# Statistics of all sixteen normalisations counted in the stages that make the rows

## The chip, the cores and the metric

The kernel runs on one core of a Trainium2 chip, as one program in fp32. The metric is the device time of one execution in microseconds (us); the median of three runs is shown.

## What is computed

A network of four layers on `x` of 128 sequences by 32 positions by 128 channels (4096 tokens of 128 values), with a second input `ctx_2048` of 128 by 257 by 256. Each layer has three blocks (cross attention, attention, feed-forward), and each of the twelve adds to `x` what it computes from the normalised `x`:

```python
def _layernorm(x, axis=-1, eps=1e-05):
    m = jnp.mean(x, axis=axis, keepdims=True)
    v = jnp.var(x, axis=axis, keepdims=True)
    return (x - m) / jnp.sqrt(v + eps)
...
    x = x + _L0_xattn_ref(_layernorm(x, axis=-1), ctx_2048, ...)
    x = x + _L0_attn_ref(_layernorm(x, axis=-1), ...)
    ...
    x = x + _L3_ffn_ref(_layernorm(x, axis=-1), L3_ffn_W1, L3_ffn_b1, L3_ffn_W2, L3_ffn_b2)
```

Some blocks normalise once more inside: the output of layer 0's cross attention, the row before layer 2's channel mixing (`x` after its RWKV recurrence), and twice in layer 2's feed-forward. That makes sixteen normalisations, each over the 128 channels of every token.

## The kernel before

The rows lie in SBUF for the whole program: `X` is 128 partitions by 32 tiles of 128 channels, a chunk is four tiles (512 columns), so there are eight chunks. `XT` holds the normalised rows turned over, channel by token, as the matmuls need them. Each block of a layer is one or more stages; a stage ends with a barrier of all engines, and buffers of a stage are its own.

`normalise` (L113 to L407) is a stage of its own, called sixteen times under the names n0x, n0y, n0a, n0f (layer 0), d1n, n1a, n1f, n2x, n2a, n2b, n2f, n2g, n2h, d3n, n3a, n3f. VectorE (DVE) runs `bn_stats` (L198) on each of the 32 tiles, which leaves six numbers per row; `variances` (L204 to L216) makes mean and variance of them in seven small instructions; ScalarE (ACT) takes the root (L334, with a warming activation at L365 and a table load ahead of it); `invert` (L227 to L240) makes the scale and one Newton step in six small instructions of DVE; then the rows are written as (x + nmean) * scale, on DVE (L250) or ACT (L346), turned over by TensorE (PE, L403) and stored to `XT` by DVE (L283, L285) or ACT (L361). This is done in two parts, tiles 0 to 15 and 16 to 31 (`PARTS`), so that the first part is written while the second is counted. The order on DVE is written out by hand:

```python
                take(*PARTS[0])
                variances(0)
                lo, hi = PARTS[1]
                take(lo, lo + 4)
                invert(0)
                take(lo + 4, hi)
                variances(1)
```

Kinds of `normalise`: with gain and bias as columns (`by_cols`, applied at the store); with gain and bias as rows (`by_rows`), where `affine` multiplies and adds them on DVE (L267, L272); with `add_to` (n0y, n2h), where POOL adds the bias rows to `X` (L315) and DVE adds the product; `whole` (n2g), which keeps the normalised rows in `H` and turns them over too; and with `keep` or `residual` and `twice` (n2a, n1f), where each tile is written a second time.

The rows that a normalisation counts were made by the stage ahead of it, always with a last addition on DVE: `mixture` (f0, f2: four `scalar_tensor_tensor` per expert at L654, f2 into `H`), `depooled` (d1, d3: L756), `layer1_attn` (m: L1007), `network` (f2a: L1191), `layer2_attn` (r: ACT stores `H` of a chunk at L1405 after `mix` of DVE, L1492 to L1508), `layer3_attn` (a: L1768), `project` (bp: L1845, into `H`), `layer2_xattn` (x), `landmark_read` (y: L3430), `gated_mixture` (g: L4400), `context_attention` (c: ACT writes `att`, L3978) and, for the first, the DMA that loads `X`, beside which `context_weights` runs. In f0, f2, d1, d3, f2a, bp, and in most of c and x, the chunks are passes of a loop, whose addresses are computed at run time. In the first normalisation SyncE (SP) issues 16 small DMAs (L3471, `store_rows`) for the next stage.

Of the kernel before, what the change touches and what calls it, by code (L numbers as in the profile page):

```python
# [20 lines left out]
ds = bass.ds  # L21

B, S, D = 128, 32, 128
TOK = B * S
P = 128
# [86 lines left out]

def normalise(k, name, src, gain=None, bias=None, twice=False, keep=None,  # L113
              add_to=None, residual=False, whole=False, eps=EPS, fetch=None):
# [6 lines left out]
    PARTS = ((0, 16), (16, TILES))  # L121
    BANKS = 4
    with ctx:
        sb, ps = buffers(nc, ctx)
        stats = sb(f"{name}_stats", [P, TILES, 6])
# [54 lines left out]

        with nc.Block() as block:
# [13 lines left out]
            def _(v):  # L195
# [46 lines left out]
                def apply(c):  # L242
# [3 lines left out]
                    if turning and c >= BANKS:  # L246
                        v.wait_ge(turned, c - BANKS + 1)
                    for t in range(TC):
                        n = c * TC + t
                        v.tensor_scalar(out[:, t], tile_of(src, n), nmean[:, n:n + 1], scale[:, n:n + 1],  # L250
                                        ALU.add, ALU.mult).then_inc(applied[c], 1)
                    if residual:
                        v.wait_ge(extra, part_of(c))
                    for t in range(TC):
# [4 lines left out]
                        elif keep is not None and twice:  # L259
# [3 lines left out]
                def affine(c):  # L263
# [22 lines left out]

                take(*PARTS[0])
                variances(0)
                lo, hi = PARTS[1]
                take(lo, lo + 4)  # L290
                invert(0)
                take(lo + 4, hi)
                variances(1)
                if by_rows or by_cols:
                    v.wait_ge(loaded, 32 if by_rows or bias else 16)
                if by_rows:
                    affine(0)
                    invert(1)
                    for c in range(1, CHUNKS):
                        affine(c)  # L300
                else:
                    apply(3)
                    invert(1)
                    apply(4)
                    store(3)
                    apply(6)
                    apply(7)
                    store(7)
# [21 lines left out]
            def _(act):  # L330
# [5 lines left out]
                def apply(c):  # L336
# [7 lines left out]
                    for t in range(TC):  # L344
                        n = c * TC + t
                        act.activation(out[:, t], tile_of(src, n), ACT.Identity, scale=scale[:, n:n + 1],  # L346
                                       bias=shift[:, 0, n:n + 1]).then_inc(applied[c], 1)
                    if both:
                        act.wait_ge(extra, part_of(c))
# [4194 lines left out]
```

## Time and profile before

| | us |
|---|---|
| median of 3 runs | 4563.62 (4560.72 to 4564.95) |
| profiled execution, whole | 4552.12 |
| its span, first to last instruction | 4550.3 |
| PE busy in the span | 3768.0 (83%) |
| DVE busy | 2792.0 (61%) |
| ACT busy | 2084.2 (46%) |
| POOL busy | 864.0 (19%) |
| mean granted clock of PE | 0.910 |

The profiled execution took 1.8 us more than its span, and 11.5 us less than the median of the runs. Busy shares are means over stages of very different kinds; PE's clock is given as a share of 2.4 GHz.

### The profile page before, as it was taken

What the parts mean: (1) busy time and instruction counts of PE and PEld (TensorE: products, weight loads), DVE (VectorE), ACT (ScalarE), POOL (GpSimd) and SP (SyncE); (2) the same over time, 40 slices, a digit from 0 to 9 for tenths busy, and PEclk for the clock granted to TensorE, in tenths of its full rate; (3) what the DMA queues carried; (4) which work ended last, traced back from release to release, by engine and by line L of the source; (5) the groups of instructions that cost most, each with busy time, mean ns of one, the idle gap of its engine ahead of it and who ended that gap; (6) DMA issues with size and microseconds to landing.
All of it is one profiled execution on the core that took longest, in us unless ns stands there. A gap on an engine that the chain in (4) does not pass through costs nothing. (4 is left out here: it accounts for less than half of the span.)

```text
span 4550.3 us, 86911 instructions
## 1 busy us (share of the span) xinstructions
PE 3768.0 (83%) x31478; PEld 2724.4 (60%) x31478; DVE 2792.0 (61%) x5475; ACT 2084.2 (46%) x4489; POOL 864.0 (19%) x832
## 2 busy tenths in 40 slices
PE   7999999999999471499996689799996777868376
PEld 6777777777777241366665356566663355646254
DVE  4666656565665686522224866477777927867783
ACT  2333333333333455444433444488887646654323
POOL 0000000000000231200001046455561022200360
PEclk8999999999999785699997889899997898989668
DMA  3111111111111145400000023122220000000000
GB/s 108 48 47 47 47 47 48 49 54 47 47 47 43 31 142 161 172 2 0 0 0 25 20 113 149 64 68 67 67 76 8 0 5 3 0 13 0 9 2 24
DMA packets 203051, 215.97 MB, mean 47 GB/s; under 512 B 37328, under 2 KB 190896, under 8 KB 195376
## 3 DMA queue, kind: packets, MB, share of 16 engines
q1 hardware_dynamic: 202800, 212.63, 14.8%
q8 instruction: 157, 2.57, 0.2%
q14 instruction: 94, 0.77, 0.1%
HBM read 185.26 MB, written 27.05 MB: 47 GB/s over the span
## 5 line engine op out<-in xcount | busy, mean ns | idle before, releaser
L3864 PE MATMUL c_psO<-c_pt,c_vc 128*128 128x512 f32 x1024 | 485.5, 596 | 2.5 <-ACT c_ot L3973 2.5
L3836 PE MATMUL c_psS<-c_kc,c_qt 128*128 128x257 f32 x2048 | 465.9, 380 | 1.1 <-DVE c_qt L4012 1.1
L3965 ACT ACTIVATE c_sc<-c_psS,c_mx 128x257 f32<-128x257 f32 x512 | 215.3, 473 | 486.6 <-DVE c_mx L4030 486.6
L3836 PEld LDWEIGHTS c_psS<-c_kc,c_qt 128*128 128x128 f32 x2048 | 381.2, 190 | 67.0 <-issue 17.5
L590 ACT ACTIVATE f_hT<-f_psH,f_b_up 128x512 f32<-128x512 f32 x320 | 214.1, 688 | 280.7 <-PE f_psH L537 275.7
L547 PEld LDWEIGHTS f_psY<-f_w_down,f_hT 128*128 128x128 f32 x2560 | 302.3, 192 | 63.9 <-issue 50.2
L537 PE MATMUL f_psH<-f_xs,f_w_up 128*128 128x512 f32 x640 | 301.5, 606 | 18.5 <-ACT f_hT L590 18.5
L3821 PEld LDWEIGHTS c_psQ<-XT,c_m 128*128 128x128 f32 x1984 | 259.8, 191 | 94.2 <-issue 90.7
L547 PE MATMUL f_psY<-f_w_down,f_hT 128*128 128x128 f32 x2560 | 305.4, 275 | 10.2 <-ACT f_hT L590 7.0
L2256 POOL TENSOR_TENSOR x_sc<-x_sc,x_rec 128x1156 f32<-128x1156 f32 x128 | 270.6, 2114 | 207.4 <-DVE x_rec L2522 207.4
L3973 ACT ACTIVATE c_ot<-c_psO 128x512 f32<-128x512 f32 x256 | 153.0, 598 | 342.3 <-PE c_psO L3864 342.3
L654 DVE SCALAR_TENSOR_TENSOR X<-f_psY,f_wt,X 128x128 f32 x256 | 72.1, 344 | 370.2 <-PE f_psY L547 370.2
L4012 DVE COPY c_qt<-c_psQ 128x512 f32<-128x512 f32 x248 | 169.4, 683 | 205.9 <-PE c_psQ L3821 205.9
L2450 ACT ACTIVATE x_sc<-x_psS,x_mx 128x289 f32<-128x289 f32 x512 | 250.0, 501 | 74.9 <-DVE x_mx L2499 74.9
L3780 POOL COPY c_z<-c_sc 128x8 f32<-128x8 f32 x128 | 24.6, 192 | 1348.3 <-DVE c_sc L4042 1348.3
L4026 DVE TENSOR_REDUCE c_nm<-c_psS 128x2 f32<-128x514 f32 x256 | 177.5, 693 | 142.9 <-PE c_psS L3836 138.3
L3821 PE MATMUL c_psQ<-XT,c_m 128*128 (+1 forms) x1984 | 261.6, 275 | 2.8 <-DVE c_qt L4012 2.8
L3864 PEld LDWEIGHTS c_psO<-c_pt,c_vc 128*128 128x128 f32 x1024 | 174.9, 190 | 133.6 <-issue 132.8
L2328 PE MATMUL x_psT<-ident,x_sc 128*128 128x128 f32 (+1 forms) x1536 | 216.4, 277 | 19.0 <-DVE x_pt L2506 12.5
L2499 DVE TENSOR_REDUCE x_mx<-x_psS 128x2 f32<-128x578 f32 x256 | 182.4, 753 | 76.6 <-PE x_psS L2313 76.4
L2328 PEld LDWEIGHTS x_psT<-ident,x_sc 128*128 128x128 f32 (+1 forms) x1536 | 159.0, 131 | 87.6 <-issue 87.4
L4255 POOL TENSOR_TENSOR g_hT<-g_gate,g_wide 128x512 f32<-128x512 f32 x128 | 173.2, 1365 | 111.7 <-ACT g_gate L4345 90.1
(816 smaller groups left out, 7683.9 us busy)
## 6 DMA issues: line engine op xcount, KB each, us to landing
c_kc<-in_ctxT SPq DMA_DIRECT2D x128, 257.0 KB
c_vc<-in_ctx SPq DMA_DIRECT2D x128, 256.0 KB
g_wide<-g_w_dram SPq DMA_DIRECT2D x32, 1024.0 KB, 8.5
x_kc<-in_ctxT SPq DMA_DIRECT2D x32, 512.0 KB
x_vc<-in_ctx SPq DMA_DIRECT2D x64, 256.0 KB
l_k_dram<-l_dist SPq DMA_DIRECT2D x32, 256.0 KB, 4.0
l_q_dram<-l_turn SPq DMA_DIRECT2D x8, 1024.0 KB, 9.8
y_pt<-l_q_dram SPq DMA_DIRECT2D x8, 1024.0 KB, 6.5
```

The source lines that it names most:

```text
L537: pe.matmul(psH[:, n % BANKS, :], w_up[:, n, :], xs[:, b, :], start=True, stop=True).then_inc(up_done, 1)
L547: mm = pe.matmul(psY[:, e % YB, t * P:(t + 1) * P], hT[:, n % SLOTS, t * P:(t + 1) * P], w_down[:, n, :], start=(u == 0), stop=(u == UT - 1))
L590: act.activation(hT[:, n % SLOTS, :], psH[:, n % BANKS, :], ACT.Gelu, bias=b_up[:, n:n + 1]).then_inc(act_done, 1)
L2256: g.tensor_tensor(sc[:, slot], sc[:, slot], bcast(rec[:, slot], 2, NK), ALU.mult).then_inc(scaled, 1)
L2328: mm = pe.transpose(psT[0:width, bank, r * P:(r + 1) * P], sc[:, c % SC, r, t * P:t * P + width], k.ident[:])
L2450: act.activation(sc[:, b % SC, r], psS[:, r, 0:NK], ACT.Exp, bias=mx[:, b % 2, r:r + 1], accum_out=sm[:, b % SC, r:r + 1]).then_inc(exp_do ...
L2499: v.tensor_reduce(two, psS[:, half * 2:half * 2 + 2, 0:NK], AX, ALU.max, negate=True)\
L3821: mm = pe.matmul(bank[:, q * P:(q + 1) * P], w["m"][:, four * 4 + q, half * P:(half + 1) * P], k.XT[:, ds(m * P, P)], start=True, stop=True)
L3836: mm = pe.matmul(psS[:, r, 0:KEYS], qt[:, b // BT, half, b % BT, r * G:(r + 1) * G].rearrange("p h i -> p (h i)"), kc[:, b // 2 % 2, b % 2 ...
L3864: mm = pe.matmul(psO[:], vc[:, slot, c % 2, t, half * P:(half + 1) * P], pt[:, c % 2, t], start=(t == 0), stop=(t == 1))
L3965: act.activation(sc[:, b % 2, r, 0:KEYS], psS[:, r, 0:KEYS], ACT.Exp, bias=mx[:, b % 2, r:r + 1]).then_inc(exp_done, 1)
L4026: v.tensor_reduce(nm[:, b % 2, two * 2:two * 2 + 2], psS[:, two * 2:two * 2 + 2, 0:KEYS], AX, ALU.max, negate=True).then_inc(reduced, 1)
```

## The change

`count_chunk` issues the four `bn_stats` of a chunk into one buffer `k.stats`, which lives as long as `X`. Every stage that makes rows calls it (or one `bn_stats` per tile, in x and c) on DVE behind its last addition to a chunk, after a wait for that addition. `normalise` is `counted=True` everywhere: it has no `bn_stats`, one part of 32 tiles, and so one `variances`, one root and one `invert`. `apply` is split into `write` (rows out) and `hold` (the second write). DVE writes chunks 0, 2, 3, 4, 6, 7 where it wrote 3, 4, 6, 7, ACT writes 1 and 5; in the `whole` kind DVE takes writes 0, 3 and 6 from ACT. The small DMAs in the first normalisation become 4 of equal total size. In layer 2's recurrence chunk j-2 is counted between `sums(j)` and `mix(j-1)`, behind a wait for ACT's store of it (`h_stored`); chunk 6 ahead of `mix(7)`, chunk 7 behind it. In `context_weights` each half of `X` is counted behind a wait for its load, ahead of the last copy of the weights (L3608 before) and of the copy of `nrow` (L3610 before). Of the thirteen places the diff below shows four; in the others the lines `v.wait_ge(added, ...)` and `count_chunk(v, k, k.X, c)` stand behind the addition named above. In `normalise` itself `affine` counts what it has added to `X` for the next one (n0a, d3n).

```diff
+def count_chunk(v, k, src, c):
+
+    for t in range(TC):
+        v.bn_stats(k.stats[:, ds(c * TC + t, 1), :], src[:, ds(c * CHUNK + t * P, P)])
...
+              add_to=None, residual=False, whole=False, eps=EPS, fetch=None, counted=True):
...
-    PARTS = ((0, 16), (16, TILES))
+    PARTS = ((0, TILES),) if counted else ((0, 16), (16, TILES))
...
-        stats = sb(f"{name}_stats", [P, TILES, 6])
+        stats = k.stats
...
+        holds = residual or (keep is not None and twice)
...
-                    v.wait_ge(stats_done, hi)
+                    if not counted:
+                        v.wait_ge(stats_done, hi)
...
+                        v.wait_ge(finished, c + 1)
+                        count_chunk(v, k, add_to, c)
...
+                    variances(0)
+                    invert(0)
+                    if by_rows:
+                        if whole:
+                            write(0)
+                        v.wait_ge(loaded, 32)
+                        for c in range(CHUNKS):
+                            affine(c)
+                            if whole and c in (0, 3):
+                                write(c + 3)
+                    else:
+                        write(0)
+                        write(2)
+                        write(3)
+                        write(4)
+                        if holds:
+                            hold(0)
+                        write(6)
+                        if by_cols:
+                            v.wait_ge(loaded, 32 if bias else 16)
+                        store(3)
+                        if holds:
+                            hold(2)
+                        write(7)
+                        if holds:
+                            hold(3)
+                            hold(6)
+                        store(7)
+                        if holds:
+                            hold(7)
...
+                elif whole:
+                    write(1)
+                    write(2)
+                    store(0)
+                    write(4)
+                    store(1)
+                    write(5)
+                    store(2)
+                    store(3)
+                    write(7)
+                    for c in range(4, CHUNKS):
+                        store(c)
+                elif by_rows:
+                    for c in range(CHUNKS):
+                        write(c)
+                else:
+                    write(1)
+                    store(0)
+                    store(1)
+                    write(5)
+                    store(2)
+                    if holds:
+                        hold(1)
+                    store(4)
+                    store(5)
+                    if holds:
+                        hold(5)
+                    store(6)
+                    if holds:
+                        hold(4)
...
+                        count_chunk(v, k, dest, c)
...
+                    if j >= 2:
+                        v.wait_ge(h_stored, j - 1)
+                        count_chunk(v, k, k.H, j - 2)
                     if j:
                         mix(j - 1)
+                v.wait_ge(h_stored, CHUNKS - 1)
+                count_chunk(v, k, k.H, CHUNKS - 2)
                 mix(CHUNKS - 1)
+                v.wait_ge(h_stored, CHUNKS)
+                count_chunk(v, k, k.H, CHUNKS - 1)
...
-                    for b in range(BT):
-                        for q in range(4):
-                            sp.dma_start(nv_dram[q, b].unsqueeze(0),
-                                         nrow[q % 2:q % 2 + 1].rearrange("o (r q d) -> o r q d", r=4, d=D)[:, :, q // 2])\
-                                .then_inc(weights_stored, 16)
-                    sp.wait_ge(weights_stored, (BT * 4 + 1) * 16)
+                    for q in range(4):
+                        row = nrow[q % 2:q % 2 + 1, q // 2 * 4 * D:(q // 2 + 1) * 4 * D]
+                        sp.dma_start(nv_dram[q].rearrange("b r d -> b (r d)").unsqueeze(0),
+                                     bcast(row, 1, BT)).then_inc(weights_stored, 16)
+                    sp.wait_ge(weights_stored, 5 * 16)
...
+                    if j == N_AT:
+                        v.wait_ge(k.x_in, 32)
+                        for c in range(CHUNKS // 2, CHUNKS):
+                            count_chunk(v, k, k.X, c)
...
+                def count_out(m):
+                    v.wait_ge(out_read, m + 1)
+                    v.bn_stats(k.stats[:, ds(m, 1), :], att[:, ds(m * D, D)])
...
+                        if b % BT == 1 and not first:
+                            count_out(m - 2)
```

**Order on DVE at the start of the first normalisation.** Before, the first ten rows of its stage; the second group of `bn_stats` lies between the two chains:

```order
L198 BN_STATS n0x_stats<-X 128x6 x16
L204 TENSOR_TENSOR n0x_diff<-n0x_stats 128x16
L205 TENSOR_TENSOR n0x_sums<-n0x_stats 128x16
L206 TENSOR_TENSOR n0x_nmean<-n0x_stats 128x16
L208 SCALAR_TENSOR_TENSOR n0x_diff<-n0x_diff 128x16
L211 SCALAR_TENSOR_TENSOR n0x_var<-n0x_sums,n0x_diff 128x16
L213 TENSOR_SCALAR n0x_nmean<-n0x_nmean 128x16
L216 TENSOR_SCALAR n0x_var<-n0x_var 128x16
L198 BN_STATS n0x_stats<-X 128x6 x4
L227 RECIPROCAL n0x_rs<-n0x_root 128x16
```

With the change, eight rows of the same stage; the chain now takes 32 columns at once:

```order
L213 TENSOR_TENSOR n0x_diff<-stats 128x32
L214 TENSOR_TENSOR n0x_sums<-stats 128x32
L215 TENSOR_TENSOR n0x_nmean<-stats 128x32
L217 SCALAR_TENSOR_TENSOR n0x_diff<-n0x_diff 128x32
L220 SCALAR_TENSOR_TENSOR n0x_var<-n0x_sums,n0x_diff 128x32
L222 TENSOR_SCALAR n0x_nmean<-n0x_nmean 128x32
L225 TENSOR_SCALAR n0x_var<-n0x_var 128x32
L236 RECIPROCAL n0x_rs<-n0x_root 128x32
```

The counting left this stage, and nothing stands between `variances` and the reciprocal.

**Order on DVE at the end of the recurrence of layer 2** (r; L1492 to L1508 are `mix`, whose lines are L1564 to L1580 with the change). Before, from the last row of `sums(7)` over `mix(6)` to the start of `mix(7)`:

```order
L1483 TENSOR_TENSOR r_past<-r_e,r_num 128x32x31
L1492 TENSOR_TENSOR r_cross<-r_lows 128x512
L1494 TENSOR_TENSOR r_ahead<-r_psU,r_lows 128x512
L1495 TENSOR_TENSOR r_back<-r_psU,r_lows 128x512
L1497 RECIPROCAL r_cross<-r_cross 128x512
L1499 TENSOR_TENSOR r_ahead<-r_ahead,r_back 128x512
L1502 SCALAR_TENSOR_TENSOR r_ahead<-r_ahead,r_sig 128x512
L1508 TENSOR_TENSOR r_mixed<-r_ahead,r_cross 128x512
L1492 TENSOR_TENSOR r_cross<-r_lows 128x512
```

With the change, the same stretch:

```order
L1555 TENSOR_TENSOR r_past<-r_e,r_num 128x32x31
L116 BN_STATS stats<-H 128x6 x4
L1564 TENSOR_TENSOR r_cross<-r_lows 128x512
L1566 TENSOR_TENSOR r_ahead<-r_psU,r_lows 128x512
L1567 TENSOR_TENSOR r_back<-r_psU,r_lows 128x512
L1569 RECIPROCAL r_cross<-r_cross 128x512
L1571 TENSOR_TENSOR r_ahead<-r_ahead,r_back 128x512
L1574 SCALAR_TENSOR_TENSOR r_ahead<-r_ahead,r_sig 128x512
L1580 TENSOR_TENSOR r_mixed<-r_ahead,r_cross 128x512
L116 BN_STATS stats<-H 128x6 x4
L1564 TENSOR_TENSOR r_cross<-r_lows 128x512
```

The count of chunk 5 came ahead of `mix(6)`, and that of chunk 6, which waits for ACT's store of it, ahead of `mix(7)`.

**Order on DVE between two chunks of f0** (ISA and REGISTER_ALU rows compute addresses of the loop; `f_lg` are the router's logits). Before:

```order
L654 SCALAR_TENSOR_TENSOR X<-f_psY,f_wt,X 128x128 x4
L603 REGISTER_ALU
L608 COPY f_lg<-f_psR 128x32
L53 ISA
L413 TENSOR_TENSOR f_gt<-f_lg 128x256
```

With the change:

```order
L719 SCALAR_TENSOR_TENSOR X<-f_psY,f_wt,X 128x128 x4
L116 ISA
L116 BN_STATS stats<-X 128x6
L116 ISA
L116 BN_STATS stats<-X 128x6
L116 ISA
L116 BN_STATS stats<-X 128x6
L116 ISA
L116 BN_STATS stats<-X 128x6
L668 REGISTER_ALU
L673 COPY f_lg<-f_psR 128x32
L53 ISA
```

The four `bn_stats` of the finished chunk, each behind a row for its address, stand ahead of the router's work for the next.

## Rows read from the trace of the kernel before

**Rows 1.** Page, busy time, share of span and instructions per engine

```profile
PE 3768.0 (83%) x31478; PEld 2724.4 (60%) x31478; DVE 2792.0 (61%) x5475; ACT 2084.2 (46%) x4489; POOL 864.0 (19%) x832
```

**Rows 2.** Line L198: idle us of DVE ahead of it, and times

```profile
  PEq L89: 24.8, 16
```

**Rows 3.** Windows: n0a, n0y, end of n0f's load, n1f, n2g, c, m, r

```profile
core 0: us, PE busy (x) PEld busy (x) DVE busy (x) ACT busy (x) POOL busy (x), PEclk, DMA share, GB/s
1529.60:1547.30 17.70, 6.80 (x32) 5.11 (x32) 15.57 (x76) 9.90 (x25) 0.00 (x0) 0.58 0.21 49
1500.00:1528.40 28.40, 0.00 (x0) 0.00 (x0) 27.58 (x74) 14.33 (x36) 9.87 (x8) 0.56 0.02 5
1932.60:1935.60 3.00, 2.48 (x12) 2.09 (x12) 2.13 (x8) 2.35 (x6) 0.00 (x0) 0.50 0.55 235
2599.20:2622.10 22.90, 7.87 (x32) 6.18 (x32) 20.32 (x94) 17.64 (x42) 0.94 (x4) 0.57 0.30 100
4029.70:4059.10 29.40, 8.92 (x32) 5.73 (x32) 20.91 (x74) 19.02 (x44) 0.00 (x0) 0.50 0.14 42
500.00:1000.00 500.00, 500.00 (x3077) 383.94 (x3076) 302.91 (x527) 164.65 (x374) 13.04 (x56) 1.00 0.16 48
2573.00:2599.00 26.00, 21.73 (x124) 16.08 (x123) 22.55 (x36) 0.16 (x1) 0.00 (x0) 0.93 0.00 0
3500.00:3650.00 150.00, 115.47 (x270) 51.64 (x270) 142.82 (x114) 99.21 (x118) 0.00 (x0) 0.89 0.00 0
```

**Rows 4.** Timeline of n0a: start, us, engine, line, operation, idle before

```profile
1529.63 3.19 DVE L198 BATCH_NORM_STATS2 n0a_stats<-X 128x6 f32<-128x128 f32 x16 [1.26 <-PEq L89]
...
1533.84 0.22 ACT L334 ACTIVATE n0a_root<-n0a_var 128x16 f32<-128x16 f32 x1 [4.02 <-DVE n0a_var L216]
...
1535.53 0.17 DVE L240 TENSOR_TENSOR n0a_shift<-n0a_nmean,n0a_rs 128x16 f32<-128x16 f32 x1
...
1535.62 2.41 DVE L198 BATCH_NORM_STATS2 n0a_stats<-X 128x6 f32<-128x128 f32 x12
1535.74 3.18 ACT L346 ACTIVATE n0a_xn<-X,n0a_shift,n0a_rs 128x128 f32<-128x128 f32 x8 [1.69 <-DVE n0a_shift L240]
...
1543.71 2.13 DVE L250 TENSOR_SCALAR n0a_xn<-X,n0a_nmean,n0a_rs 128x128 f32<-128x128 f32 x8
...
1546.60 0.69 DVE L285 COPY XT<-n0a_psT 128x512 f32<-128x512 f32 x1 [0.75 <-PE n0a_psT L403]
```

**Rows 5.** Timeline of n0x and of the end of context_weights

```profile
28.71 1.21 DVE L3610 COPY d_nrow<-d_psW 2x1024 f32<-2x1024 f32 x1 [2.79 <-PE d_psW L3571]
...
30.66 1.28 ACT L365 ACT_TABLE_LOAD   x1 [3.57 <-PEq L89]
...
31.43 11.51 SPq L3471 DMA_DIRECT2D c_nv_dram<-d_nrow  x16
31.95 0.20 ACT L365 ACTIVATE n0x_root<-ident 1x1 f32<-1x1 f32 x1
```

**Rows 6.** Timeline of n0y while POOL adds the bias rows

```profile
1503.39 3.77 POOL L315 TENSOR_TENSOR X<-X,n0y_rows 128x512 f32<-128x512 f32 x3 [19.63 <-DMA n0y_rows<-in_L_xattn_ln_bias]
...
1504.83 1.12 DVE L211 SCALAR_TENSOR_TENSOR n0y_var<-n0y_sums,n0y_diff 128x16 f32<-128x16 f32 x1
...
1507.11 0.86 DVE L198 BATCH_NORM_STATS2 n0y_stats<-c_att 128x6 f32<-128x128 f32 x4
```

**Rows 7.** Timeline of f0 between two chunks

```profile
2002.57 1.12 DVE L654 SCALAR_TENSOR_TENSOR X<-f_psY,f_wt,X 128x128 f32 x4 [2.45 <-PE f_psY L547]
...
2009.54 1.55 PE L537 MATMUL f_psH<-f_xs,f_w_up 128*128 128x512 f32 x3 [2.68 <-ACT f_hT L590]
```

**Rows 8.** Timeline of r around the start of `mix(7)`

```profile
3638.41 0.69 DVE L1492 TENSOR_TENSOR r_cross<-r_lows 128x512 f32<-128x512 f32 x1
...
3639.55 0.60 ACT L1405 ACTIVATE H<-r_psO 128x512 f32<-128x512 f32 x1 [4.59 <-PE r_psO L1343]
```

**Rows 9.** Timeline of y (behind an addition) and of bp

```profile
1897.05 0.23 DVE L3413 TENSOR_SCALAR y_rec<-y_psO 128x64 f32<-128x64 f32 x1 [1.21 <-PE y_psO L3386]
...
4018.63 0.69 DVE L1841 TENSOR_TENSOR bp_rows<-bp_psP,bp_b_row 128x512 f32<-128x512 f32 x1 [0.18 <-PE bp_psP L1828]
```

More of the change, by code:

```diff
@@ L245, in apply @@
                     v.wait_ge(scale_done, part_of(c))
-                    if turning and c >= BANKS:
+                    if turning and not whole and c >= BANKS:
                         v.wait_ge(turned, c - BANKS + 1)
@@ L334, in roots, with write @@
                     act.activation(root[:, used, lo:hi], var2[:, used, lo:hi], ACT.Sqrt).then_inc(root_done, 1)
-                def apply(c):
+                def write(c):
                     out = rows_out(c)
@@ L354, in apply @@
                                            bias=shift[:, 1, n:n + 1])
-                        elif keep is not None and twice:
+                        else:
                             act.activation(tile_of(keep, n), tile_of(src, n), ACT.Identity, scale=rstd[:, n:n + 1],
@@ L369, in _ @@
                     act.wait_ge(loaded, 32 if bias else 16)
-                if by_rows:
-                    for c in range(CHUNKS):
-                        apply(c)
-                        if c == 1:
-                            roots(1)
-                        if turning and c:
-                            store(c - 1)
-                    if turning:
-                        store(CHUNKS - 1)
-                else:
-                    apply(0)
-                    apply(1)
+                if not counted:
+                    write(0)
+                    write(1)
                     store(0)
                     roots(1)
-                    apply(2)
+                    write(2)
                     store(1)
                     store(2)
-                    apply(5)
+                    write(5)
                     store(4)
@@ L390, in _ @@
                     store(6)
+                elif whole:
+                    write(1)
+                    write(2)
+                    store(0)
+                    write(4)
+                    store(1)
+                    write(5)
+                    store(2)
+                    store(3)
+                    write(7)
+                    for c in range(4, CHUNKS):
[3 more added lines that the diff above has]
+                        write(c)
+                else:
+                    write(1)
+                    store(0)
+                    store(1)
+                    write(5)
+                    store(2)
[8 more added lines that the diff above has]
+                        hold(4)
             if turning:
@@ L2528, in add @@
                     v.tensor_tensor(at, at, psA[:, 0:D], ALU.add).then_inc(added, 1)
+                    v.wait_ge(added, m + 1)
+                    v.bn_stats(k.stats[:, ds(m, 1), :], at)
                 def chunk(i, h, first, last):
```

67 lines of the change are left out of this document (42 added, 25 removed).

## The prediction

> **What bounds the kernel now.** The page's first part comes first: PE is busy for 83% of the span and DVE for 61% [rows 1]. These are means over stages that a barrier keeps apart, so they do not say what a DVE instruction is worth. For that I read the sixteen normalisations as stages. DVE stood idle ahead of the counting line sixteen times, each time for the barrier alone [rows 2]. The windows of rows 3 show what goes on inside: in n0a DVE is busy for 15.57 of 17.70 us, PE for 6.80. The timeline of n0a gives the chain [rows 4]: 16 tiles are counted in 3.19 us, the root starts 4.21 us after the stage, DVE's chain behind it ends 1.86 us later (1533.84 to 1535.70), ACT writes its first rows 6.1 us after the start, and the last store ends at 1547.29, 17.66 us after the start. Nothing else of the kernel runs meanwhile. So the counting is paid at full price there, and the question is what it costs where it goes. For that I read the end of a chunk in each stage that makes rows, and ask whether DVE's next instruction was waiting for somebody (the count is free), or others wait for DVE (the count is paid again).
>
> **Savings: the normalisations.** Without counting, `variances` needs 1533.84 - 1532.82 = 1.02 us (from the end of the first 16 counts to the root); with 32 columns I take 1.15. But twelve of the sixteen stages begin with a table load on ACT, 1.28 us, and a warming activation of 0.20 [rows 5], so the root can't start before 1.5. From the root to the scale is 1.86, so rows are written from 3.35 on, where it was 6.1. DVE then writes six chunks at 1.11 (two take 2.13, and there are gaps) and stores one at 0.75 before its last write ends, and from there to the end of the last store it takes 1.45 (1545.84 to 1547.29): 3.35 + 6.66 + 0.75 + 1.45 = 12.2. Against 17.7 that is **5.5 us less** in n0x, n0f, d1n, n2x, n2b, n2f, n3f, and 5.85 in n0a, n1a, d3n, n3a, which load no table: 38.5 + 23.4 = 61.9. At this point a rule speaks against the change.
>
> On the row first: the warming activation starts at 31.95, 1.29 us after the load's start [rows 5], so load and root follow each other at once. The Trainium skill ("ScalarE: Activation LUTs", section "What ACT_TABLE_LOAD costs") adds about 1.38 us of drain to each switch; by that the root would come at 2.9 in twelve stages and the sum would be 16.6 us worse. The sum goes by the row, and the rule is a rival below.
>
> n1f and n2a write every tile twice. In n1f DVE is busy for 20.32 of 22.90 [rows 3]; 6.5 of counting and some 2.1 of the second chain (of 1.02 + 1.86, less the root's part) leave, two writes and a hold (3.3) come: **6.5 less** each, 13. n2g is bound by ACT, which wrote and stored all eight chunks (19.02 busy) [rows 3]; it now begins at 3.35 with five writes of 1.6 (eight tiles: 3.18 [rows 4]) and eight stores of 0.6 (as L1405 in rows 8), and with a tail estimated at 3 it makes 19.2 of 29.4: **10 less**.
>
> n0y and n2h add to `X`. DVE needs per chunk two passes of 0.69 and the next stage's count of 0.82, with the gaps some 2.45: from 5.1 us on this makes 24.7, against 28.4 [rows 3]. But POOL's eight additions lie beside it, and rows 6 show what that does: a DVE instruction on 16 columns took 1.12 us (0.17 in rows 4 for one like it), while four `bn_stats` took 0.86 as elsewhere. Before, this hit small instructions only; now it hits the 0.69 passes, for about the first three chunks. If each waits for a POOL addition (3.77 for three) that adds 5: 29.7. I take 28.9, **0.5 more** each, near the upper end since the row stands at this very place; the ends are -3.7 and +1.3. The Trainium skill ("SBUF — State Buffer", "SBUF: two separate sides") says the same in general: DVE with two SBUF inputs and GpSimd exclude each other for a whole instruction. If one took the pair as free, each stage would be 3.7 faster.
>
> Savings together: 61.9 + 13 + 10 - 1 = **83.9**.
>
> **Costs: the stages that make rows.** A chunk's count is 3.19 / 4 = 0.80 to 0.86 us [rows 4, 6] and the wait for the addition some 0.1: 0.95. Where addresses are computed in a loop, the nearest row is four `scalar_tensor_tensor` in 1.12 [rows 7], so 0.95 to 1.15.
> - *Serial with the critical engine.* In f0 the count stands between the last mix and the router's logits, and PE waited 2.68 us for what follows from them [rows 7]: eight times 0.95 = 7.6. f2 is built alike: 7.6. bp: DVE waits 0.18 ahead of its next addition [rows 9], so eight times 1.0 = 8. m: DVE is busy for 22.55 of 26 us [rows 3], eight times 0.95 less some gaps of about 0.5: 6.3.
> - *r*, the recurrence: DVE is busy for 142.82 of 150 [rows 3]. Six counts of 0.85 are 5.1. Ahead of `mix(7)`, DVE waits for ACT's store of chunk 6, which ends at 3640.15, and counts to 3641.0, where `mix(7)` began at 3638.41 [rows 8]: 2.6. The last count hides behind PE and ACT's store of `X`. Together 7.7: more than n2b saves, 5.5.
> - *Gaps that hold a part.* In y DVE waited 1.21 us for PE behind an addition [rows 9], which hides a count, but not in the last chunks and not in all others: 4.5 (ends 1 and 7.6). a and g I put at 2.5 each with the ends 1 and 7.6, a chunk being free or paid.
> - *Only the tail.* In c PE is busy for 500 of 500 us and DVE for 302.91 [rows 3]: one count of 0.28 per tile falls into DVE's idle time, 0.5 at the end. f2a 1.1, d1 and d3 1.2 each (behind the last addition), x 0.5: 4.5 in all. If the cover in c were gone, 32 counts of 0.3 are 10.
> - *context_weights*: 16 counts of 3.3 us go ahead of each of two copies, and DVE was idle for 2.79 ahead of the copy of `nrow` [rows 5]: 1.1 late.
> - *Transfers.* f0's weights still load at 1932.6 to 1935.6, at a share of 0.55 of these 3 us, so they land some 13.7 us after the start [rows 3]; f0 could now start at 13.2: with the semaphore 0.9 late. SP's 16 DMAs in n0x (11.51 us, from 31.43 [rows 5]) end at 42.94, about where n0x now ends (30.7 + 12.2); four instead end by 35, so SP is free. Buffers, branches and the rest: nothing.
>
> Costs together: 7.6 + 7.6 + 8 + 6.3 + 7.7 + 4.5 + 5 + 4.5 + 1.1 + 0.9 = **53.2**.
>
> **The sum.** 53.2 - 83.9 = -30.7: the profiled execution of 4552.1 (its span of 4550.3 and 1.8 around it, which stays) would take 4521.4. That execution lies 11.5 under the median; the median 4563.6 becomes **4533** (-0.67%). A measurement of this kernel tells about 0.2% (9 us) from no change.
>
> **Rivals.**
> 1. *The counts find gaps.* For it: 39% of DVE's time is idle [rows 1], and y's 1.21. Against it: the waits of f0, r, bp. If y, a, g and m give back what their lower ends allow (8) and POOL leaves n0y and n2h alone (8.4), it is 17 less: 4516. Chance 0.22.
> 2. *The counts are paid everywhere, POOL's lock too.* y, a, g at their upper ends (+13), n0y and n2h (+1.6), loops at 1.15 (+5): 4553. Chance 0.12.
> 3. *The root waits longer for its table.* Before, the root came 4.2 us after the start and any wait behind the load was covered; if it is now held for as long again as the load takes, twelve stages lose 1.28: +15.4, so 4548. For it: the cover of counting is gone. Against it: the warming activation follows the load at once [rows 5]. Chance 0.03. The page of the Trainium skill named above gives 1.38 for the same wait, which makes 4550.
> 4. *Slower: addresses.* Each `bn_stats` of a loop stands behind an instruction for its address, and has two addresses that move. In f0, f2, bp and, past a gap like y's 1.21 [rows 9], in d1 and d3 this is 40 chunks. If one tile costs 0.6 us or more in place of 0.24, a chunk costs 2.4: +1.45 in 24 chunks, +1.2 in 16, and c and x, with 64 single counts of which half might then be exposed at 0.3, +10: 35 + 19 + 10 = 64, so 4597. With f0, f2, bp, d1 and d3 alone the gain is gone at about 0.46 us per tile. Against it: rows 7, a like row, at 0.28. Chance 0.05.
> 5. *It does nothing net*, because gaps fail and loops are dearer at once (+30): 4563. Chance 0.05.
>
> The forecast itself, 4533 within 8, has 0.53.
>
> **Range and chances.** 4506 to 4554: downwards to rival 1 and 10 below it, the most that n1f, n2a, n2g and r may give beyond my terms; upwards past rivals 2 and 3. Outside lie 4 and 5 and some of each end. Faster by over 0.2% (under 4554.5) is 0.53 + 0.22 + most of 2 and 3 = 0.88; within 0.2% 0.06; slower 0.06.
>
> **What would show it.** Line L198 is gone; 32 counts per stage appear in the stages that make rows. n0a's window is about 11.9 us, n0f's 12.2, n1f's 16.4, n2g's 19.2, n0y's 28.9. In f0 PE's wait at the chunk's end is 3.6 in place of 2.68; in r the store of chunk 6 ends ahead of a count and `mix(7)` begins 2.6 us behind it. The prediction is wrong in its mechanism if the normalisations shrink by less than 4 us, or if the stages that make rows do not grow; it is wrong in size if y, a, g, m take other parts than above, or if n0y falls well under 28.

## The result, and the profile after

| | before | after |
|---|---|---|
| median, us | 4562.17 (4552.76 to 4564.95, 4 runs) | 4506.86 (4501.13 to 4508.48, 4 runs) |
| ratio | | 0.9882, 95% interval 0.9868 to 0.9895 |
| profiled execution, span | 4552.1, 4550.3 | 4505.6, 4503.9 |
| PE, DVE, ACT busy | 3768.0, 2792.0, 2084.2 | 3772.2, 2798.1, 2036.6 |

A second comparison on another chip gave 0.9897 (0.9878 to 0.9915). The kernel is 55 us faster by the medians and 46 by the profiled executions; 31 were forecast, and 4506.86 lies at the very end of the range.

The page of the changed kernel, first part, answers to [rows 1]: DVE did not work less, it worked elsewhere.

```profile
PE 3772.2 (84%) x31478; PEld 2730.1 (61%) x31478; DVE 2798.1 (62%) x5389; ACT 2036.6 (45%) x4349; POOL 866.1 (19%) x829
```

The windows of n0a, n0y, n1f and n2g, and of two chunks of f0, in the changed kernel; they answer to [rows 3]:

```profile
1524.80:1535.90 11.10, 5.69 (x32) 4.85 (x32) 9.74 (x39) 6.75 (x16) 0.00 (x0) 0.69 0.32 78
1496.50:1522.70 26.20, 0.00 (x0) 0.00 (x0) 22.92 (x57) 14.41 (x35) 12.51 (x8) 0.52 0.02 5
2589.40:2605.50 16.10, 6.91 (x32) 6.00 (x32) 15.19 (x60) 13.10 (x29) 0.52 (x2) 0.62 0.39 143
4009.60:4028.50 18.90, 8.92 (x32) 5.72 (x32) 15.77 (x41) 14.11 (x31) 0.00 (x0) 0.50 0.22 65
2240.60:2305.70 65.10, 61.71 (x340) 44.03 (x340) 15.04 (x52) 24.46 (x36) 0.62 (x1) 0.95 0.00 0
2305.70:2367.90 62.20, 58.93 (x340) 42.94 (x340) 14.94 (x52) 24.28 (x36) 0.00 (x0) 1.00 0.00 0
```

The first four are 17.70, 28.40, 22.90 and 29.40 us long in the kernel before. The last two are passes of one loop with the same instructions, 2.9 us apart in time and 0.05 in granted clock; this comes back below.

The timeline of n0a in the changed kernel, to set beside [rows 4]:

```profile
1524.82 0.21 DVE L213 TENSOR_TENSOR n0a_diff<-stats 128x32 f32<-128x32 f32 x1 [1.24 <-PEq L89]
...
1525.92 0.23 ACT L374 ACTIVATE n0a_root<-n0a_var 128x32 f32<-128x32 f32 x1 [0.92 <-DVE n0a_var L225]
...
1527.58 5.24 DVE L259 TENSOR_SCALAR n0a_xn<-X,n0a_nmean,n0a_rs 128x128 f32<-128x128 f32 x20
1527.69 1.65 ACT L386 ACTIVATE n0a_xn<-X,n0a_shift,n0a_rs 128x128 f32<-128x128 f32 x4 [1.54 <-DVE n0a_shift L249]
...
1532.73 0.68 DVE L299 COPY XT<-n0a_psT 128x512 f32<-128x512 f32 x1
...
1533.33 1.10 DVE L259 TENSOR_SCALAR n0a_xn<-X,n0a_nmean,n0a_rs 128x128 f32<-128x128 f32 x4
...
1535.19 0.69 DVE L299 COPY XT<-n0a_psT 128x512 f32<-128x512 f32 x1 [0.75 <-PE n0a_psT L468]
```

Rows are written 2.76 us after DVE's first instruction (6.1 after the start before), and DVE writes 20 tiles in one stretch of 5.24 us.

Where the time went, stage by stage, is a subtraction of two timelines: a normalisation from its first instruction (the table load where it has one) to the end of its last, a maker (a stage that makes rows) from there to the next normalisation. Us, of four profiled executions (the second of each kernel is from the experiments):

| stage | before | again | after | again |
|---|---|---|---|---|
| n0a (n1a, n3a, d3n within 1.0) | 17.7 | 17.7 | 11.1 | 11.1 |
| n0f (with a table load; n0x, n2x, n2b, n2f, n3f within 0.6, d1n 18.7 before) | 17.8 | 17.7 | 11.5 | 11.5 |
| n1f / n2a | 22.8 / 23.2 | 22.8 / 23.0 | 16.2 / 16.3 | 16.2 / 16.3 |
| n2g | 29.4 | 29.4 | 18.9 | 19.0 |
| n0y / n2h | 28.4 / 28.4 | 28.4 / 27.4 | 26.2 / 26.1 | 26.2 / 26.3 |
| all sixteen, change against the same column before | | | -99.5 | -100.1 |
| f0 | 497.2 | 510.1 | 512.3 | 511.4 |
| m | 100.5 | 100.5 | 109.0 | 107.8 |
| r | 179.2 | 181.2 | 189.4 | 189.3 |
| batch attention and bp | 257.6 | 258.1 | 266.3 | 266.2 |
| f2 | 158.4 | 158.2 | 164.5 | 164.5 |
| layer 0's attention with y | 373.3 | 374.9 | 369.7 | 372.7 |
| layer 3's attention (a) | 134.4 | 128.6 | 132.9 | 132.5 |
| all else (makers and what lies between), the same | | | +53.1 | +40.8 |

By the first pair of profiles, 99.5 came out of the normalisations and 53.1 went into the makers. The second pair agrees on the first of these and not on the second: f0 alone differs by 12.9 between the two executions of the kernel before.

### The profile page after: what moved, and what is told of

Its sections match the earlier page's. It is cut to its first block and busy times, and to the rows that moved or that the text cites. A ratio compares the mean times of both kernels' runs of the same rounds, so it can differ in the third digit from the quotient of the medians.

```text
span 4503.9 us, 87030 instructions
## 1 busy us (share of the span) xinstructions
PE 3772.2 (84%) x31478; PEld 2730.1 (61%) x31478; DVE 2798.1 (62%) x5389; ACT 2036.6 (45%) x4349; POOL 866.1 (19%) x829
## 3 DMA queue, kind: packets, MB, share of 16 engines
q1 hardware_dynamic: 202704, 212.63, 14.9%
## 5 line engine op out<-in xcount | busy, mean ns | idle before, releaser
L2411 PEld LDWEIGHTS x_psT<-ident,x_sc 128*128 128x128 f32 (+1 forms) x1536 | 159.5, 131 | 87.5 <-issue 87.3
L602 PEld LDWEIGHTS f_psH<-f_xs,f_w_up 128*128 128x128 f32 x640 | 117.7, 198 | 138.7 <-issue 101.6
```

Source lines behind the costliest of these rows:

```text
L602: pe.matmul(psH[:, n % BANKS, :], w_up[:, n, :], xs[:, b, :], start=True, stop=True).then_inc(up_done, 1)
L2411: mm = pe.transpose(psT[0:width, bank, r * P:(r + 1) * P], sc[:, c % SC, r, t * P:t * P + width], k.ident[:])
```

## The experiments

Theory A, mine: a gain is what counting costs inside a normalisation, less what it costs where DVE is waited for. The rival B: the new division of the writes, which the diff brings along, makes the gain.

**a_here.** All counting at the start of each normalisation. `count_chunk` returns at once, so that the makers count nothing, but the waits ahead of the counts stay in them.

```diff
                 else:
+                    take(0, TILES)
+                    v.wait_ge(stats_done, TILES)
                     variances(0)
```

> All 32 statistics are counted at the start of each of the sixteen normalisations again, in one part, and no stage that makes rows counts; the new order of writes, the single chain and the 4 DMAs stay. Theory A (the gain is the difference between what counting costs in a normalisation and in the makers): against the changed kernel each normalisation grows by 6.5 us less the wait for the table load, 5.9 (6.5 in the four that load none), 97 in all, and the makers shrink by their 53, so it is 44 slower than the change, about 4551, near the kernel before; a normalisation like n0f takes about 17.4 where the kernel before has 17.8. Rival B (the single chain and the new order of writes do most of it): n0f takes 15 or less and the kernel is 20 or more under the one before, 4540 or less.

Measured: 4550.56 (4543.18 to 4557.40, 9 runs) beside 4557.45 for the kernel before, ratio 0.9982 (0.9972 to 0.9992). n0f took 17.4, n0a 17.4, n1f 22.2, n2g 24.9. The makers went back most of the way: m 101.9, r 183.3, f2 159.5, bp 261.0, still 1.3, 3.1, 1.2 and 3.1 above the mean of the kernel before, with the waits and no count. So the restructuring without moved counts, these waits included, is worth 7 us; n2g alone gave 4.5. Rival B falls as it was put (n0f at 15 or less, 20 us in all). But this shows one side of the matter only: what the new order of writes is worth while DVE counts.

**j_split.** The counting stays outside, the eleven plain and by-column normalisations divide their chunks as before.

```diff
+                    elif not holds:
+                        write(3)
+                        write(4)
...
+                        store(3)
+                        write(6)
+                        write(7)
+                        store(7)
                     else:
...
+                elif not holds:
+                    write(0)
+                    write(1)
+                    store(0)
+                    write(2)
...
```

> The eleven plain and by-column normalisations keep the counting outside and the single chain, but the chunks are divided between DVE and ACT as in the kernel before (DVE writes 3, 4, 6, 7, ACT 0, 1, 2, 5). Theory B' (half the gain inside a normalisation is the new division): ACT has four writes of 1.65 and six stores of 0.6 from 3.1 us on, 13.3 and a tail, so n0f takes about 14 where the change has 11.5. Rival A' (the counting alone makes the gain): n0f stays at 11.5 to 12.

Measured: one execution, 4545.78 (the kernel before on its chip 4553.50 to 4563.84), a span of 4544.0, 40 us over the change's profile; the eleven stages took 14.3 to 16.0, n0f 14.7, n0a 14.9. Its timeline of n0a:

```profile
1530.08 1.11 DVE L259 TENSOR_SCALAR n0a_xn<-X,n0a_nmean,n0a_rs 128x128 f32<-128x128 f32 x4
1530.19 3.19 ACT L395 ACTIVATE n0a_xn<-X,n0a_shift,n0a_rs 128x128 f32<-128x128 f32 x8 [1.54 <-DVE n0a_shift L249]
...
1533.15 1.12 DVE L259 TENSOR_SCALAR n0a_xn<-X,n0a_nmean,n0a_rs 128x128 f32<-128x128 f32 x4 [1.96 <-PE n0a_psT L488]
...
1537.46 0.69 DVE L299 COPY XT<-n0a_psT 128x512 f32<-128x512 f32 x1 [3.19 <-PE n0a_psT L488]
```

DVE, free of counting, now waits: 1.96 us for a bank and 3.19 for chunk 3's turn, since chunks 0, 1 and 2 come out of ACT in 3.19 us for two, with its stores between. The four values for n0a are: counting inside, old division 17.7; inside, new 17.4; outside, old 14.9; outside, new 11.1. The last two differ in the division alone: it is worth 3.8 us once the counting is gone. The first two differ in the single chain of `variances` and `invert` as well, so the 0.3 between them is both together, and no run takes them apart. Of the 71.1 us that the eleven stages lost, 40.5 need the division as well.

**b_mid.** f0 and f2 count the finished chunk inside the next; for this the first pass of DVE's loop is written out ahead of the loop (not shown).

```diff
                             v.wait_ge(mixed, c * E + e + 1 + YB)
+                            if e == 4 and not (first and b == 0):
+                                count_chunk(v, k, dest, c - 1)
...
-                        count_chunk(v, k, dest, c)
+                count_chunk(v, k, dest, CHUNKS - 1)
```

> f0 and f2 count a finished chunk in the middle of the next one, behind the fifth expert's mix, where DVE waits for PE; the last chunk behind the loop. Theory A (the count lengthens PE's wait between chunks, and the longer wait also costs granted clock in some chunks): f0's chunks go from 62.2 to 65.1 us each back to 61.3 to 61.8, the clock in each is 1.00 again, f0 is 10 to 12 shorter and f2 5 to 6, together 16 under the change, about 4491. Rival C (the address instructions of the loop cost, wherever they stand): f0 stays within 3 us of the change. Rival D (the clock fell by chance): f0's chunks go to 62.3 less 0.9 = 61.4 at 1.00 clock, but an unchanged kernel would show such chunks too; told apart by the next run.

Measured: 4496.34 (4491.71 to 4498.43, 4 runs), ratio 0.9860 (0.9844 to 0.9877), some 10 under the change. f0's two chunks at clock 1.00 took 61.3 (the first, which counts nothing) and 61.5 us, where the change has 62.2 to 62.4: the count is hidden, 0.8 a chunk. But six chunks ran at 0.97, 61.5 to 63.4 us, and f0 lost only 3 (509.2). Most of f2's chunks stayed at 19.7 to 20.0 (f2 163.3, 1.2 less): DVE is busy for 15.5 us of each, and behind the moved count its next twelve additions follow without a gap (3.61 us), so that the count delays them where it stands now. Theory A holds for the count in f0 and fails for the clock and f2.

**c_double.** A second count per chunk of f0, into an unread buffer.

```diff
                         count_chunk(v, k, dest, c)
+                        if name == "f0":
+                            for t in range(TC):
+                                v.bn_stats(k.twice[:, ds(c * TC + t, 1), :], dest[:, ds(c * CHUNK + t * P, P)])
```

> f0 counts each finished chunk twice (the second time into a buffer that nobody reads), all else as in the change. Theory A: PE's wait between chunks grows from about 3.2 to 4.1 us, by 0.85 per chunk, and the granted clock falls in nearly all chunks, where in the change it fell in three of seven: f0 grows by 7 for the counts and by 4 to 8 more for the clock, 11 to 15 over the change. Rival D (the fall of the clock is chance, not PE's wait): 7 more, with about as many chunks under 1.00 as before.

Measured: one execution, 4527.68; f0 525.0, 12.7 over the change. Seven of its chunks were at 0.95 to 0.97; the first, at 1.00, took 62.9. PE's wait between two chunks in the changed kernel, and with the second count:

```profile
2116.69 3.70 PE L602 MATMUL f_psH<-f_xs,f_w_up 128*128 128x512 f32 x8 [3.22 <-ACT f_hT L655]
...
2179.02 5.40 PE L602 MATMUL f_psH<-f_xs,f_w_up 128*128 128x512 f32 x8 [3.40 <-ACT f_hT L655]
```

```profile
2126.00 5.40 PE L602 MATMUL f_psH<-f_xs,f_w_up 128*128 128x512 f32 x8 [4.00 <-ACT f_hT L655]
```

The wait grew by 0.6 to 0.8, as a count should make it. Eight matmuls behind it take 3.70 us in one chunk and 5.40 in another: there the clock is at its lower level for a while. The 12.7 us lie in theory A's range, but how much of them is the clock's, and whether the count caused that, this run can't say; the next one bears on it.

**before_again.** The kernel before, once more.

> The kernel before once more, for the spread of stages that a change did not touch. In its first profile all chunks of f0 ran at a granted clock of 0.99 to 1.00, 61.3 to 61.8 us each; with the counting taken out of f0 again (a_here) five chunks showed 0.97 and 63.0 to 63.3. Theory D (the low chunks are chance in both kernels): this profile shows some of them too, f0 at 500 to 507 where the first had 497.2, and layer 0's attention between 366 and 374. Theory A (only the changed kernels have them): f0 within 1 us of 497.2, all chunks at 0.99 or more.

Measured: 4563.74, span 4561.9, and f0 at 510.1. Three of its chunks:

```profile
1945.20:2006.80 61.60, 60.98 (x345) 43.49 (x343) 14.19 (x48) 24.24 (x35) 0.62 (x1) 1.00 0.00 1
2006.80:2070.40 63.60, 60.62 (x340) 43.53 (x340) 14.18 (x48) 24.40 (x36) 0.62 (x1) 0.97 0.00 1
2070.40:2134.80 64.40, 61.99 (x340) 44.07 (x340) 14.18 (x48) 24.44 (x36) 0.62 (x1) 0.95 0.00 0
```

Theory D was right: chunks at the low clock are in the kernel before as well (seven of eight here), and its first profile happened to have none. Against this execution f0 grew by 2.2 and not by 15.1. Layer 3's attention moved by 5.8 the other way with no edit. The two profiled executions lie 11.6 us apart, and f0's 12.9 is most of what moved. That the 11.5 us between the first profile and the median have this cause is likely; no profile shows the other runs.

**d_three.** m, r and bp don't count; n1f, n2b, n2g count at their start (the three `count_chunk` sites out, `take` in as in a_here).

> Layer 1's attention (m), layer 2's recurrence (r) and the projection (bp) do not count; n1f, n2b and n2g count their 32 tiles at their own start. In the profiles m grew by 8.4, r by 10.1, bp by 8.7 with the change. Theory A (DVE is the critical engine there, so the count costs more than the 5.9 it saves): 27.2 come back, 17.7 are paid: 9.5 under the change, about 4497; in r mix(7) begins with no wait for ACT's store, and the last matmuls run at the higher clock again (0.88 where the change has 0.65). Rival E (part of these 27 is chance, as with the 6 us that a stage without any edit lost): less than 3 under the change.

Measured: 4500.16 (4494.72 to 4506.11, 4 runs), ratio 0.9873 (0.9857 to 0.9890); the span 4496.5, 7.4 under the change's profile. m with n1f: 124.9, where the changed kernel has 125.2 and 124.0: nothing. (m itself took 102.7 with neither counts nor waits, 2.1 over the kernel before; no run shows why.) r with n2b: 198.1 for 201.1. Batch attention, bp and n2g: 281.5 for 285.2. So counting in m pays for itself and no more, and r and bp lose 3 and 3.7. Of the 9.5 expected 7 are in these stages. The last matmuls of r run at the higher clock again, as theory A said: the eight on `r_mixed` wait 0.40 us and take 1.16, where the change has 4.16 and 2.07, and over the last 15 us of r the granted clock is 1.00 against 0.64. e_rlate asks whether the wait is what decides it.

**e_rlate.** Chunk 6 is counted behind `mix(7)`.

```diff
-                v.wait_ge(h_stored, CHUNKS - 1)
-                count_chunk(v, k, k.H, CHUNKS - 2)
                 mix(CHUNKS - 1)
+                v.wait_ge(h_stored, CHUNKS - 1)
+                count_chunk(v, k, k.H, CHUNKS - 2)
```

> In the recurrence chunk 6 is counted behind mix(7) instead of ahead of it, all else as in the change. Theory A: mix(7) starts 2.6 us earlier, at once behind mix(6), and PE's wait for it is shorter, so the granted clock of the last stretch rises from 0.65 towards 0.88: r falls from 189.4 to 185.6 (of the 10.1 it grew, 4.7 stay for six counts). Rival E (the wait for ACT's store costs nothing, r grew by chance): r stays within 1 us of 189.4, which three profiles have shown (189.4, 189.5, 189.3).

Measured: one execution, 4500.52; r 186.8, 2.5 less than the change where 3.8 were expected. The changed kernel has, to set beside [rows 8]:

```profile
3618.23 0.60 ACT L1477 ACTIVATE H<-r_psO 128x512 f32<-128x512 f32 x1 [5.37 <-PE r_psO L1415]
...
3618.86 0.87 DVE L116 BATCH_NORM_STATS2 stats<-H 128x6 f32<-128x128 f32 x4 [1.88 <-ACT H L1477]
...
3619.65 0.67 DVE L1564 TENSOR_TENSOR r_cross<-r_lows 128x512 f32<-128x512 f32 x1
...
3626.83 2.07 PE L1415 MATMUL r_psO<-r_w_out,r_mixed 128*128 128x128 f32 x8 [4.16 <-DVE r_mixed L1580]
```

and this kernel:

```profile
3615.58 0.69 DVE L1564 TENSOR_TENSOR r_cross<-r_lows 128x512 f32<-128x512 f32 x1
...
3622.64 0.86 DVE L116 BATCH_NORM_STATS2 stats<-H 128x6 f32<-128x128 f32 x4
3622.78 2.08 PE L1415 MATMUL r_psO<-r_w_out,r_mixed 128*128 128x128 f32 x8 [1.61 <-DVE r_mixed L1580]
```

In the changed kernel DVE waits 1.88 for ACT's store and counts ahead of the critical mix: 1.88 + 0.79. Here `mix(7)` follows at once. a_here shows the wait by itself: DVE waits the same 1.88 us there with nothing to count, and r is 3.1 above the kernel before. Eight matmuls at the end still take 2.08 us, where both profiles of the kernel before had 1.16 behind the same wait of PE, 1.61: so PE's wait just ahead of them does not decide their clock, and what does stays open. Over the last 15 us of r the granted clock is 0.77, between 0.64 with the change and 0.89 before. Theory A holds for DVE's wait, whose 2.6 came back as 2.5, and for the clock at most by halves.

**f_nobias.** POOL's additions of the bias rows in n0y and n2h are left out, with them the two biases of the output.

```diff
                         for c in range(CHUNKS):
-                            add_bias(c)
+                            g.sem_inc(biased, 1)
```

> n0y and n2h leave out POOL's additions of the bias rows to X; the output lacks these two biases. Theory F (POOL and DVE exclude each other while both read two tiles of SBUF): DVE's passes take 0.69 throughout where they took up to 1.64, and n0y goes from 26.2 to 3.1 + 1.7 + 8 x 2.22 = 22.6, n2h from 26.1 to the same. Rival G (ACT's writes or the chain on DVE itself set the time, POOL is covered): both stay within 1 us of 26.

Measured: one execution, 4491.59; n0y 22.0 and n2h 22.0 (26.2 and 26.1 with the change). The changed kernel's n0y:

```profile
1500.00 12.51 POOL L355 TENSOR_TENSOR X<-X,n0y_rows 128x512 f32<-128x512 f32 x8 [20.45 <-DMA n0y_rows<-in_L_xattn_ln_bias]
1501.51 1.52 DVE L279 TENSOR_TENSOR n0y_xn<-n0y_xn,n0y_rows 128x512 f32<-128x512 f32 x1 [1.79 <-ACT n0y_xn L386]
1503.06 1.64 DVE L284 TENSOR_TENSOR X<-X,n0y_xn 128x512 f32<-128x512 f32 x1
1504.74 0.87 DVE L116 BATCH_NORM_STATS2 stats<-X 128x6 f32<-128x128 f32 x4
1505.53 0.85 DVE L279 TENSOR_TENSOR n0y_xn<-n0y_xn,n0y_rows 128x512 f32<-128x512 f32 x1
```

and without POOL:

```profile
1499.74 0.69 DVE L279 TENSOR_TENSOR n0y_xn<-n0y_xn,n0y_rows 128x512 f32<-128x512 f32 x1 [1.79 <-ACT n0y_xn L386]
1500.47 0.69 DVE L284 TENSOR_TENSOR X<-X,n0y_xn 128x512 f32<-128x512 f32 x1
1501.19 0.87 DVE L116 BATCH_NORM_STATS2 stats<-X 128x6 f32<-128x128 f32 x4
```

Passes of 0.69 become 1.52, 1.64 and 0.85, POOL's eight additions 12.51 us where they took 9.87 [rows 3], and `bn_stats` takes 0.87 in both. DVE's passes follow one another without a gap, so it is the passes that grew and not a wait for POOL's semaphore. Theory F is right: 4.1 us a stage.

**k_best** and **l_best** put together what paid: b_mid, e_rlate, bp without counting (n2g's own), and the bias of n0y added by POOL at the start of the context attention, which does not touch `X`; k_best also adds n2h's bias behind f2's loop.

```diff
             def _(g):
+                add_early(k, g, bias_row, bias_in)
                 g.wait_ge(fixed, 9 * 16)
```

> A version out of the runs so far: f0 and f2 count a chunk in the middle of the next; chunk 6 of the recurrence is counted behind mix(7); the projection does not count and n2g does at its own start; POOL adds the bias rows of n0y and n2h to X in the stages ahead (at the start of layer 0's context attention and at the end of f2, where POOL has little to do) instead of beside DVE's passes. Against the changed kernel: f0 -5 (0.75 for each of seven chunks), r -2.6, bp and n2g together -3.7, n0y and n2h -4.1 each as without the bias: 19 less, about 4488 where the change has 4507. Rival: POOL's additions at the start of the context attention or behind f2's loop delay these stages by their 9.9 us each: 10 to 20 of it are lost, 4497 to 4507.

> As k_best, but POOL adds the bias rows of n2h beside DVE's passes again, as in the change; those of n0y stay in layer 0's context attention. In k_best POOL's additions behind f2's loop made its last chunk 26.4 us where the others take 19.8 (f2 170.8 for 163.3 in b_mid), and n2h gained 4.1. Theory: f2 returns to 163.5, n2h to 26.1: 3.3 under k_best, about 4490. Rival: the last chunk of f2 was long for another reason, and f2 stays at 170: 4497.

Measured: k_best 4493.07 (4485.27 to 4497.55, 5 runs), ratio 0.9859 (0.9840 to 0.9877); l_best 4488.46 (4481.74 to 4489.77, 5 runs), ratio **0.9840** (0.9827 to 0.9854), the lowest median of all, 69 us under the kernel before on its chip. Both intervals overlap with that of b_mid alone (0.9860): k_best is no faster than b_mid by these runs, though the stages it edits beyond it gained some 14 and lost 7 in f2, and that l_best beats b_mid is likely rather than shown. In k_best one chunk of f2 shows POOL at work beside DVE's router:

```profile
4131.23:4157.60 26.37, 18.51 (x100) 13.32 (x99) 21.27 (x55) 8.08 (x12) 9.20 (x7) 0.87 0.00 0
4157.60:4178.21 20.61, 15.19 (x90) 10.97 (x88) 15.73 (x56) 6.82 (x11) 0.00 (x0) 0.96 0.00 0
```

DVE is busy for 21.27 us there, some 15.6 in other chunks, and the granted clock falls to 0.87. So k_best's rival came for f2, by 7.4 us (170.8 for b_mid's 163.3), and not for the context attention, which took 1451.3 in both versions: POOL's work at its start costs nothing. In l_best f2 is back at 163.5 and n2h at 26.1, as expected.

**after_again.** The changed kernel beside k_best.

> The changed kernel once more, beside the version above on the same chip: 4507 within 6, ratio 0.988 to the kernel before. In the profile the chunks of f0 show a granted clock under 0.99 in two to five of eight, n0f takes 11.5, the recurrence 189.3; layer 0's attention lies between 366 and 375 and layer 3's between 128 and 136.

Measured: 4510.55 (4504.37 to 4513.66, 5 runs), ratio 0.9897 (0.9878 to 0.9915); f0 511.4 with four chunks at 0.97, n0f 11.5, r 189.3, layer 0's attention 372.7. Within the expected ranges, the median 3.7 over the first.

## Why the prediction was right or wrong

The direction, the mechanism and the range held; the size was 55 where 31 was said. Of the 24 us between them, 15.6 lie in the normalisations (9.2 in the eleven plain ones, 1.0 in n1f, n2a and n2g, 5.4 in n0y and n2h) and 9 in the execution that the sum started from. The makers' sum was met by luck. Step by step:

- *Plain normalisations*, "5.5 us less" and 5.85: measured 5.9 to 7.0, together 71.1 where 61.9 stood. The stage of 12.2 was 11.5. Each factor was a little high: the first write at 3.14 and 2.76 (3.35 and 3.0 said), six chunks at 1.06 (1.11), 0.5 for the store (0.75); the tail of 1.45 was right.
- *But their cause was told wrongly by halves.* The sum used the new division ("DVE then writes six chunks") without saying what it was worth. j_split shows it: 40.5 of the 71.1 are gone without it. "Without counting" and with the single chain alone the eleven stages give 30.6, and the one execution of such a kernel took 4545.8, 12 us under the kernel before on its chip.
- *n1f, n2a, n2g*: -6.7, -6.9 and -10.4 where 6.5, 6.5 and 10 stood. For n1f the working doesn't give its number: 6.5 and 2.1 less, 3.3 more make 5.3. DVE's busy time did fall by 5.1 (20.32 to 15.19); the rest was idle time of DVE, which the working doesn't have. So 6.5 was right by luck.
- *n0y and n2h*, "0.5 more each": with its last count, which the table has in the row behind it, n0y took 27.1 where 28.9 was said and 28.4 were before, 1.3 less. The exclusion of DVE and POOL cost 4.1, not 5, and a chunk without it takes 2.24 (1499.74 to 1501.98 in f_nobias), not 2.45: 5.05 + 8 x 2.24 + 4.1 = 27.1. The step that failed is "with the gaps some 2.45".
- *The rule on the shared pair* (the Trainium skill, "SBUF — State Buffer", "SBUF: two separate sides"): the trace agrees with the exclusion, 1.52 and 1.64 for 0.69; that `bn_stats`, with one input, stays at 0.87 us for four fits it too.
- *The rule on the table load* (the Trainium skill, "ScalarE: Activation LUTs", "What ACT_TABLE_LOAD costs"): the root came 1.52 us after the start of n0f (1905.60, 1907.12), not 2.9. The trace disagrees: no drain of 1.38 is seen behind a load ahead of which ACT was idle. The measurement decides, and rival 3 fell.
- *Makers*, 53.2 said, 53.1 measured by the first pair, and yet not right: f0's +15.1 holds about 5.6 of counts (0.7 a chunk), 1.6 for the weights, and the rest is the clock of one execution. By the second pair it is 40.8 (there the kernel before had seven low chunks and the changed one four, so what the change costs lies between). The single terms, by the means of the two profiles of each kernel: m +7.9 (6.3 said, 1.3 of it taken off for gaps that the runs don't show), r +9.1 (7.7), batch attention with bp +8.4 (8), f2 +6.2 (7.6), d1 +1.5 and d3 +0.8 (1.2 each), g +1.2 (2.5), a within its chance of some 6 us (2.5). f0 was 7.6 said for counts: about 5.6; PE's wait at a chunk's end grew from 2.4 to 2.9 us to 3.2 to 3.5, by 0.6 to 0.8 and not by 0.9.
- *Transfers*: f0 waited for its weights as foreseen, and longer than 0.9:

```profile
1920.56 1.28 ACT L643 ACT_TABLE_LOAD   x1 [4.54 <-DMA f_w_down<-in_L_ffn_wd]
```

  The start of f0's work lay 2.3 us behind the barrier (POOL began at 1918.22).
- *y* (4.5 said): from its first reciprocal to the next stage 36.7 became 39.2, +2.5. The rest of layer 0's attention, which nobody touched, was 6.1 shorter in this pair, and no term of the sum has that. It is hardly chance alone: this rest took 336.6 and 336.7 in the two profiles of the kernel before and 328.1 to 333.9 in the eleven others, also in a_here (330.3), where nothing is counted in it. Some 3 to 8 us thus seem to come with the edits that a_here shares with the change; no run takes these apart.
- *r*, "more than n2b saves": r +9.1 to 10.1, n2b -6.5. Right, and d_three and e_rlate give 3 and 2.5 of it back.
- *The base.* The profiled execution of the kernel before was taken as a fair one, 11.5 under the median. It was the fastest of the kernel's five executions up to the result, with no low clock in f0. A sum against it carries over to the median only if that chance stays out. The changed kernel's profile had no such luck (1.2 under its median), which is the difference between 46 and 55.

Rival 1, gaps for the counts, was nearest in result (4516) and partly in mechanism: g and y gave back 1.3 and 2, n0y and n2h some 1.8 each. Rivals 2, 4 and 5 did not come, nor did the wait of rival 3. That 4506.86 still lies inside the range, 0.86 from its end, owes something to luck: the 15.6 us missed in the normalisations nearly used up the 17 of rival 1, and the base took the rest.

What stays open: what decides whether a chunk of f0 falls to the low clock. It happened in none to seven of eight chunks of the same code, with PE waits of 2.4 to 4.0 us between chunks; c_double, with the longest waits, had seven, and the kernel before had as many in its second profile with waits of 2.42 to 2.89, the waits of its first. The same question stands at the end of r. Nor is it shown what makes the rest of layer 0's attention, ahead of y, shorter in every version than in the kernel before.

## What to carry to other kernels

Moving work off a stage where an engine is alone with it pays in full only when the stage is then divided anew: here 2.8 us of n0a's 6.6 came with the counting gone (and the chain made single), 3.8 more from giving the freed engine its share. At the other end, ask of each place whether the next instruction there is waited for: counting cost 0.7 to 1.1 us a chunk where it was, moved counts cost nothing in f0 where DVE waited, and one wait for another engine's store with the count behind it, put ahead of a critical chain, cost as much as three counts. Profile the unchanged kernel twice before subtracting stages.

## What was not expected of the hardware

- One and the same loop pass of f0 took 61.4 to 64.4 us in the kernel before and 62.2 to 65.1 in the changed one, with the granted clock at 1.00 to 0.95 of 2.4 GHz. Two executions of the kernel before differ by 12.9 us in f0 and by 11.6 as a whole, a fifth of this change.
- A `tensor_tensor` of DVE with two SBUF inputs took 1.52 to 1.64 us for 0.69 beside POOL's, and POOL's went from 1.23 to 1.56 each (12.51 for eight), while four `bn_stats` stayed at 0.87: here the statistics were work that DVE did beside POOL at no cost.
- POOL's additions beside f2's router raised one chunk from 19.8 to 26.4 us and f2 by 7.4, more than the 4.1 they had cost in n2h.
